# Mamba block of a macaron network: the causal mask of the decay factors moves into spare rows of the cumulative sums' products

## The chip, the cores and the metric

The kernel runs on one core of a Trainium2 chip, in one launch. The metric is the device time of that launch in microseconds (us), taken as the median of three runs. TensorE (PE, with its weight loads PEld), VectorE (DVE), ScalarE (ACT), GpSimd (POOL) and SyncE (SP) each run their own stream of instructions and wait for one another on semaphores. A difference under about 2% is about what these runs can't tell from none.

## The reference

A macaron layer: half a mixture of experts, then a Mamba-2 mixer, then the mixture of experts again, each behind a layer norm and with a residual. The input is 2 x 2048 tokens of width 256. The part that the change touches is the mixer's recurrence over the tokens:

```python
x = x + 0.5 * ffn(layernorm(x))
x = x + mamba2(layernorm(x))      # 8 heads of width 64, state 64
x = x + 0.5 * ffn(layernorm(x))

# inside mamba2, token by token
dA = exp(dt * A)
s = s * dA_t[..., None, None] + dt_t * x_t (outer) B_t
y = einsum('bhpn,bn->bhp', s, C_t)
```

## The kernel before

The program is three blocks behind one another, with a barrier of all engines between two: `ffn_block`, `mamba_block`, `ffn_block`. The change is in `mamba_block` alone, which runs from about 375 us to 905 us of the profiled execution.

`mamba_block` takes the 4096 tokens as 32 tiles (chunks) of 128, in 8 groups of four (`GC = 4`). It computes the recurrence in its chunked form. With `cum` the cumulative sum of `dt * A` within a chunk, the output at token t takes from token s <= t of the same chunk the factor `exp(cum_t - cum_s)` times the product B_s C_t. For each head this factor is a 128 x 128 matrix with s on the partitions and t along the columns, and everything with s > t must vanish.

The order of the work is written out by hand. Each engine has one Python loop `for s in SLOTS` (from -10 to 34), and in slot `s` it works on several tiles at once: TensorE's `within(s)` and `from_state(s)` for tile s, `sums(s + 1, ...)`, `turn_b(s + 1)` and `turn_xc(s + 1)` for tile s + 1, `turn_x(s + 9)` for the normalised input nine tiles ahead. The `project` calls (the five convolution blocks of a group) stand at places that tables give: `EARLY` ones in slots 0 and 1 of every four, ahead of `sums(s + 1, 1)`; `LATE` ones in slots 3, 0 and 1, behind `project_z`. Slots -10 to -1 are a lead-in that only normalises, transposes and projects tiles. Steps hand over by counting semaphores (`Step`), so an engine never runs ahead of what its wait names, and does everything in program order.

The steps that the argument follows:

- `sums(i, half)` on TensorE fills the PSUM bank `pE` for four heads: four products of 128 columns (L1389), whose stationary operand is one column of the selection matrix `pick` broadcast over 128 columns (96 partitions: the high, middle and low bfloat16 parts of 32 rows of cumulative sums in `cumT`), and one product of 512 columns (L1391), an identity times the constant `future`, which adds -1e30 wherever s > t. It runs twice for a tile: `half` 0 at the head of the slot ahead of `from_state`, `half` 1 behind `turn_xc` and an early `project`, ahead of `turn_x` and `turn_y`.
- `decay(i, half)` on ScalarE takes the exponential of `pE` into `ex` (L1245).
- `copy_b(i)` on ScalarE copies the product of B and C and the transposed B into `GB` (L1228).
- `mask(i)` on VectorE multiplies `ex` (all 8 heads, 1024 columns) by that product (L1623). `within(i)` on TensorE then uses `ex` as eight stationary operands (L1340).
- `gate_y(i)` and `add_skip(i)` on GpSimd work on the output `yv` (L1122, L1117), `scale_x` on the inputs of the next tile (L1130 to L1132). `powers(s)` computes `rstd` of the layer norms (L1106); `shift` on VectorE (L1539) and `norm` on ScalarE (L1177) wait for it.
- The start of GpSimd's stream in this block builds the constants with memsets and selects, chained by semaphore waits. TensorE (and VectorE in `prepare`) waits for the last of them, and `powers` stands behind them on GpSimd.
- `softplus(G)` on VectorE is a chain of small operations once for each group (L1569 to L1578), and TensorE's sums over a group (L1476) wait for it.

## Time and profile before

| | us |
|---|---|
| three runs | 1271.49, 1258.30, 1272.85 |
| median | 1271.49 |
| profiled execution: span from first to last instruction | 1265.8 |
| median less that span | 5.7 |
| first `ffn_block`, to the last work of its kind | 0 to 369 |
| `mamba_block` | 375 to 905 |
| second `ffn_block` | 905 to 1265.8 |

The profile has the span of the profiled execution and no other time for it. The stages are read off the timeline of instructions. All durations below come from this one execution.

### The profile page before, as it was taken

How to read it: one execution, taken by the hardware profiler on the slowest of the kernel's cores; microseconds unless marked ns; L12 is line 12 of the kernel's file. 1: busy time of each engine (PE TensorE's matmuls, PEld its weight loads, DVE VectorE, ACT ScalarE, POOL GpSimd, SP SyncE). 2: the span in 40 equal slices, each digit the busy share in tenths (PEclk: the TensorE clock that was granted, in tenths of full speed). 3: DMA queues.
4: the chain of work that ended last, by engine and by line, in shares of the span. 5: the costliest groups of instructions: out<-in, count | busy, mean ns of one | idle time of the engine just before them, and what ended most of it. 6: DMA issues, size and time to landing. Idle time of an engine off the chain costs nothing. (4 is left out here: it accounts for less than half of the span.)

```text
span 1265.8 us, 21732 instructions
## 1 busy us (share of the span) xinstructions
PE 1050.3 (83%) x6532; PEld 870.1 (69%) x6532; DVE 748.1 (59%) x1614; ACT 605.8 (48%) x1560; POOL 607.9 (48%) x612
## 2 busy tenths in 40 slices
PE   3746999999965788989898888989836999999960
PEld 2745999999954556666676666657525999999950
DVE  5974444444427778677878786865355444444437
ACT  1323555555533455556555656565314555555530
POOL 6922555555531245354545454647502555555520
PEclk9997999999985598899989989999858999999985
DMA  7872222322313101111111110000061232222339
GB/s 227 276 294 74 76 76 76 99 76 76 76 59 93 38 30 43 42 42 42 43 42 42 43 38 17 27 17 21 22 279 38 88 97 92 94 95 91 100 117 327
DMA packets 73258, 112.20 MB, mean 89 GB/s; under 512 B 10680, under 2 KB 60352, under 8 KB 71872
## 3 DMA queue, kind: packets, MB, share of 16 engines
q1 hardware_dynamic: 48704, 60.48, 14.2%
q0 software_dynamic: 13824, 37.77, 9.3%
q10 hardware_dynamic: 10624, 12.58, 2.9%
q8 instruction: 61, 1.00, 0.3%
q14 instruction: 45, 0.37, 0.1%
HBM read 66.76 MB, written 44.04 MB: 88 GB/s over the span
## 5 line engine op out<-in xcount | busy, mean ns | idle before, releaser
L427 POOL DMA_INDIRECT ys_d<-xs,row_of x144 | 142.4, 989 | 195.6 <-DVE xs L811 188.2
L422 POOL DMA_INDIRECT xs<-xn_d,token_of x144 | 140.1, 973 | 115.1 <-DVE token_of L785 71.8
L491 ACT ACTIVATE hs<-pH 128x512 f32<-128x512 f32 x144 | 86.0, 597 | 227.6 <-PE pH L613 217.6
L800 DVE TENSOR_TENSOR xl<-pT,xh 128x256 fp32r<-128x256 f32 x144 | 61.1, 424 | 212.7 <-PE pH L613 108.7
L805 DVE TENSOR_TENSOR h2l<-hs,h2h 128x512 fp32r<-128x512 f32 x144 | 99.8, 693 | 81.3 <-ACT h2h L499 77.3
L1604 DVE SCALAR_TENSOR_TENSOR acc<-bank,cwh,acc 128x511 f32<-128x511 f32 (+2 forms) x120 | 89.6, 747 | 40.5 <-ACT acc L1218 37.7
L633 PE MATMUL pY<-w2h,h2h 128*128 x576 | 103.5, 302 | 1.4 <-DVE h2l L805 1.2
L1122 POOL TENSOR_TENSOR yv<-yv,sz 128x512 f32<-128x512 f32 x32 | 40.7, 1272 | 120.6 <-DVE yv L1643 117.4
L613 PE MATMUL pH<-w1h,xh 128*128 x288 | 93.0, 405 | 1.8 <-DVE xl L800 1.1
L613 PE MATMUL pH<-w1l,xh 128*128 x288 | 92.3, 402 | 0.0
L633 PE MATMUL pY<-w2h,h2l 128*128 x576 | 91.1, 280 | 0.0
L613 PE MATMUL pH<-w1h,xl 128*128 x288 | 90.9, 397 | 0.0
L633 PE MATMUL pY<-w2l,h2h 128*128 x576 | 89.5, 278 | 0.0
L497 ACT ACTIVATE hs<-pR 128x512 f32<-128x512 f32 x144 | 87.3, 606 | 4.2 <-PE pR L622 4.2
L499 ACT ACTIVATE h2h<-pR 128x512 fp32r<-128x512 f32 x144 | 89.0, 618 | 0.0
L622 PE MATMUL pR<-ident,hs 128*128 128x128 f32 x576 | 86.3, 272 | 0.0
L633 PEld LDWEIGHTS pY<-w2h,h2h 128*128 128x128 f32 x576 | 78.2, 190 | 2.5 <-issue 2.5
L1106 POOL TENSOR_TENSOR m_rstd<-m_ve,neghalf 128x3 f32<-128x3 f32 x43 | 41.1, 956 | 76.2 <-DVE m_ve L1533 76.2
L633 PEld LDWEIGHTS pY<-w2h,h2l 128*128 128x128 f32 x576 | 77.5, 188 | 0.0
L633 PEld LDWEIGHTS pY<-w2l,h2h 128*128 128x128 f32 x576 | 76.9, 188 | 0.0
L1316 PE MATMUL bank<-wo,yT 128*128 128x256 f32 x256 | 74.0, 440 | 0.0
L1245 ACT ACTIVATE ex<-bank,dts 128x128 f32<-128x128 f32 x256 | 73.3, 380 | 0.6 <-PE bank L1391 0.6
(250 smaller groups left out, 2591.4 us busy)
## 6 DMA issues: line engine op xcount, KB each, us to landing
m_yg<-ys_d SPq DMA_DIRECT2D x64, 128.0 KB, 2.1
xs<-ys_d SPq DMA_DIRECT2D x12, 512.0 KB, 6.8
wst<-in_L_ffn_w_dram ACTq DMA_DIRECT2D x8, 512.0 KB, 4.6
xs<-in_L_attn_x_dram SPq DMA_DIRECT2D x8, 512.0 KB, 6.5
hs<-in_L_ffn_w_dram ACTq DMA_DIRECT2D x8, 512.0 KB, 4.7
xn_d<-xs SPq DMA_DIRECT2D x8, 512.0 KB, 3.4
lo_d<-w1l SPq DMA_DIRECT2D x1, 4096.0 KB, 11.8
lo_d<-w2l SPq DMA_DIRECT2D x1, 4096.0 KB, 21.4
```

What stands on the lines that cost most here:

```text
L422: pool.indirect_dma_start(out=xg[:, t % NX, :], out_offset=None, in_=xn_d, in_offset=bass.IndirectOffsetOnAxis(ap=token_of[:, t:t + 1], ax ...
L427: pool.indirect_dma_start(out=ys_d, out_offset=bass.IndirectOffsetOnAxis(ap=row_of[:, t:t + 1], axis=0), in_=y[:, t % NX, :], in_offset=No ...
L491: act.activation(r[:, u, :], pH[u][:, :], ACT.Relu).then_inc(relu_done.sem, 1)
L497: act.activation(h2[:, u, :, :], turned_h, ACT.Square)
L499: act.activation(h2h[:, u, :, :], turned_h, ACT.Square).then_inc(sq_done.sem, 1)
L613: last = pe.matmul(pH[u][:, :], a[:, u, k, :], w[:, k * HID:(k + 1) * HID], start=(n == 0), stop=(n == 3 * KD - 1))
L622: last = pe.transpose(pR[u][:, k * P:(k + 1) * P], r[:, u, k * P:(k + 1) * P], ident[:, :])
L633: last = pe.matmul(pY[u][:, 0:D], a[:, u, k, :], w[:, k * D:(k + 1) * D], start=(n == 0), stop=(n == 3 * KH - 1))
L805: dve.tensor_tensor(h2l[:, u, :, :], h2[:, u, :, :], h2h[:, u, :, :].bitcast(F32), ALU.subtract).then_inc(h2_split.sem, 1)
L1245: last = act.activation(ex[:, i % 2, h, :], pE[:, n * P:(n + 1) * P], ACT.Exp, bias=dts[:, G % 3, NCUM, k * H + h:k * H + h + 1])
L1316: last = pe.matmul(out, a, b, start=(m == 0), stop=(m == len(parts) - 1))
L1604: ins = dve.scalar_tensor_tensor(a, bank[:, 0:GT - n], cwh[:, b, HALO - n:HALO - n + 1], a, ALU.mult, ALU.add)
```

## The change

The block loses two constants (`ident_bf`, `future`) and the 512-column product L1391. In their place:

- `cumT` gets 32 more partitions, 96 to 127. Row 96 + r holds -1e30 in columns 4r to 4r + 3 and zero elsewhere. They are written once.
- `pick` is no longer 96 x 32 with a broadcast at the time of use, but is written out whole: 128 partitions x 32 selections x 128 columns. In partitions 96 to 127 row r holds one from column 4(r + 1) on. The product of the two thus adds -1e30 where s lies in a later run of four tokens than t, within the same four products of 128 columns.
- What is left to mask are the diagonal 4 x 4 blocks. A new step on GpSimd, `keep_past`, sets the B C product in `GB` to zero where s > t, once for each tile, between `gate_y` of the tile before and `scale_x`. `mask` waits for it.
- `mask` becomes one operation of two stages, the minimum with 3e38 and then the product, since the exponential of an unmasked positive difference could be infinite.

```diff
--- before.py
+++ after.py
@@ -883,6 +883,7 @@
 TAPPED = {0: (1, 0), 1: (1, 2), 2: (1, 4)}
 HANDED = {1: (1, 1), 2: (1, 3)}
 HALO = CONV - 1
+RUN = P // 32
 RX = 14
 LEAD = 10
 
@@ -923,9 +924,8 @@
         heads = sb("heads", [P, 3, H])
         negA, bias = sb("negA", [P, GC, H]), sb("m_bias", [P, GC, H])
         CH = GC * H
-        ident_bf, future = sb("ident_bf", [P, P], BF16), sb("future", [P, GC, P], BF16)
-        pick = sb("pick", [3 * CH, CH], BF16)
-        cumT, rest, mid = sb("cumT", [3 * CH, 2, P], BF16), sb("m_rest", [CH, 2, P]), sb("m_mid", [CH, P], BF16)
+        pick = sb("pick", [P, CH, P], BF16)
+        cumT, rest, mid = sb("cumT", [P, 2, P], BF16), sb("m_rest", [CH, 2, P]), sb("m_mid", [CH, P], BF16)
         xr = sb("xr", [P, RX, D])
         yg = sb("m_yg", [P, 2, TOP, D])
         st, st2 = sb("m_st", [P, 6]), sb("m_st2", [P, 6])
...
@@ -1079,18 +1079,20 @@
         @block.gpsimd
         def _(pool):
             chain = Chain(pool, consts)
-            pool.memset(ident_bf[:, :], 0.0)
-            pool.memset(future[:, :, :], 0.0)
             pool.memset(S[:, :], 0.0)
-            chain.link(pool.memset(pick[:, :], 0.0))
+            chain.link(pool.memset(pick[:, :, :], 0.0))
             for part in range(3):
-                chain.link(pool.affine_select(out=pick[:, :], in_=pick[:, :], compare_op=ALU.not_equal, fill=1.0,
-                                              base=-part * CH, pattern=[[-1, CH]], channel_multiplier=1))
-            chain.link(pool.affine_select(out=ident_bf[:, :], in_=ident_bf[:, :], compare_op=ALU.not_equal, fill=1.0,
-                                          base=0, pattern=[[-1, P]], channel_multiplier=1))
-            chain.link(pool.affine_select(out=future[:, :, :], in_=future[:, :, :], compare_op=ALU.is_ge, fill=-1e30,
-                                          base=0, pattern=[[0, GC], [1, P]], channel_multiplier=-1))
-            for s in (pow_done, xdt_done, xw_done, s1_done, td_done, yv_done, h_ready):
+                chain.link(pool.affine_select(out=pick[0:3 * CH, :, :], in_=pick[0:3 * CH, :, :], compare_op=ALU.not_equal, fill=1.0,
+                                              base=-part * CH, pattern=[[-1, CH], [0, P]], channel_multiplier=1))
+            last = 3 * CH
+            chain.link(pool.memset(pick[last:P, :, :], 1.0))
+            chain.link(pool.memset(cumT[last:P, :, :], -1e30))
+            chain.link(pool.affine_select(out=pick[last:P, :, :], in_=pick[last:P, :, :], compare_op=ALU.is_ge, fill=0.0,
+                                          base=-RUN, pattern=[[0, CH], [1, P]], channel_multiplier=-RUN))
+            for edge, sign in ((0, 1), (RUN - 1, -1)):
+                chain.link(pool.affine_select(out=cumT[last:P, :, :], in_=cumT[last:P, :, :], compare_op=ALU.is_ge, fill=0.0,
+                                              base=edge, pattern=[[0, 2], [sign, P]], channel_multiplier=-sign * RUN))
+            for s in (pow_done, past_done, xdt_done, xw_done, s1_done, td_done, yv_done, h_ready):
                 s.open(pool)
 
             def powers(s):
@@ -1120,6 +1122,11 @@
                 pool.wait_ge(sz_done.sem, sz_done.done(i))
                 pool.wait_ge(t2_done.sem, t2_done.done(i))
                 pool.tensor_tensor(yv[:, :], yv[:, :], sz[:, i % 2, :], ALU.mult).then_inc(yv_done.sem, 1)
+
+            def keep_past(i):
+                pool.wait_ge(bt_done.sem, bt_done.done(i))
+                pool.affine_select(out=GB[:, 0:P], in_=GB[:, 0:P], compare_op=ALU.is_ge, fill=0.0,
+                                   base=0, pattern=[[1, P]], channel_multiplier=-1).then_inc(past_done.sem, 1)
 
             def scale_x(i):
 
@@ -1154,6 +1161,7 @@
                     add_skip(s)
                     gate_y(s)
                 if live(s + 1):
+                    keep_past(s + 1)
                     scale_x(s + 1)
                 if rooted(s + 1):
                     powers(s + 1)
@@ -1308,7 +1316,7 @@
             for s in (xT_ready, x2T_ready, logit_ready, z_ready, dt_ready, cum_ready, p_ready, turned, sm_ready, e0_ready, e1_ready, i_ready, y_ready, s_ready,
                       yT_ready, o_ready):
                 s.open(pe)
-            pe.wait_ge(consts, 6)
+            pe.wait_ge(consts, 9)
 
             def product(out, parts):
 
@@ -1386,10 +1394,9 @@
                     pe.wait_ge(ex0_done.sem, ex0_done.done(i))
                 for n in range(GC):
                     col = k * H + half * GC + n
-                    pe.matmul(pE[:, n * P:(n + 1) * P], pick[:, col:col + 1].to_broadcast([3 * CH, P]), cumT[:, G % 2, :],
-                              start=(n == 0), stop=False, skip_group_check=True)
-                pe.matmul(pE[:, :], ident_bf[:, :], future[:, :, :].rearrange("p h t -> p (h t)"),
-                          start=False, stop=True, skip_group_check=True).then_inc((e0_ready, e1_ready)[half].sem, 1)
+                    last = pe.matmul(pE[:, n * P:(n + 1) * P], pick[:, col, :], cumT[:, G % 2, :],
+                                     start=True, stop=True)
+                last.then_inc((e0_ready, e1_ready)[half].sem, 1)
 
             def turn_x(i):
                 pe.wait_ge(norm_done.sem, norm_done.done(i))
@@ -1487,7 +1494,7 @@
             def prepare():
 
                 dve.wait_ge(loads, 5 * 16)
-                dve.wait_ge(consts, 6)
+                dve.wait_ge(consts, 9)
                 link(dve.tensor_scalar(cwh[:, :, :], cw[:, :, :], 0.5, None, ALU.mult))
                 link(dve.tensor_scalar(cbh[:, :], cb[:, :], 0.5, None, ALU.mult))
                 dve.wait_ge(a_prep, 1)
@@ -1620,7 +1627,9 @@
 
             def mask(i):
                 dve.wait_ge(ex_done.sem, ex_done.done(i))
-                dve.tensor_tensor(ex[:, i % 2, :, :], ex[:, i % 2, :, :], GB[:, 0:P].rearrange("p (a t) -> p a t", a=1).to_broadcast([P, H, P]), ALU.mult).then_inc(M_done.sem, 1)
+                dve.wait_ge(past_done.sem, past_done.done(i))
+                past = GB[:, 0:P].rearrange("p (a t) -> p a t", a=1).to_broadcast([P, H, P])
+                dve.scalar_tensor_tensor(ex[:, i % 2, :, :], ex[:, i % 2, :, :], BIG, past, ALU.min, ALU.mult).then_inc(M_done.sem, 1)
 
             def scale_state(i):
                 dve.wait_ge(i_ready.sem, i_ready.done(i))
```

On GpSimd, at the start of the block (`pick` and `cumT` are the operands of `sums`; m_rstd is what `powers` writes), before:

```order
L1082 MEMSET ident_bf 128x128
L1083 MEMSET future 128x512
L1084 MEMSET S 64x512
L1085 MEMSET pick 96x32
L1087 AFFINE_SELECT pick<-pick 96x32 x3
L1089 AFFINE_SELECT ident_bf<-ident_bf 128x128
L1091 AFFINE_SELECT future<-future 128x512
L1106 TENSOR_TENSOR m_rstd<-m_ve,neghalf 128x3 x9
```

and with the change:

```order
L1082 MEMSET S 64x512
L1083 MEMSET pick 128x4096
L1085 AFFINE_SELECT pick<-pick 96x4096 x3
L1088 MEMSET pick 32x4096
L1089 MEMSET cumT 32x256
L1090 AFFINE_SELECT pick<-pick 32x4096
L1093 AFFINE_SELECT cumT<-cumT 32x256 x2
L1108 TENSOR_TENSOR m_rstd<-m_ve,neghalf 128x3 x9
L1147 TENSOR_TENSOR hc<-hsave,cwh 128x15
```

The selects on `pick` have become selects of 4096 columns, and they stand ahead of the first `powers` as the small ones did.

On GpSimd, in the steady part, one tile's work (`yv` is the output, GB the B C product), before:

```order
L1112 TENSOR_TENSOR S<-S,dts 64x512
L1117 TENSOR_TENSOR yv<-yv,xD 128x512
L1122 TENSOR_TENSOR yv<-yv,sz 128x512
L1130 TENSOR_TENSOR xdt<-xt,dts 128x512
L1131 TENSOR_TENSOR xD<-xt,heads 128x512
L1132 TENSOR_TENSOR xt<-xt,dts 128x512
L1106 TENSOR_TENSOR m_rstd<-m_ve,neghalf 128x3
```

and with the change:

```order
L1114 TENSOR_TENSOR S<-S,dts 64x512
L1119 TENSOR_TENSOR yv<-yv,xD 128x512
L1124 TENSOR_TENSOR yv<-yv,sz 128x512
L1128 AFFINE_SELECT GB<-GB 128x128
L1137 TENSOR_TENSOR xdt<-xt,dts 128x512
L1138 TENSOR_TENSOR xD<-xt,heads 128x512
L1139 TENSOR_TENSOR xt<-xt,dts 128x512
L1108 TENSOR_TENSOR m_rstd<-m_ve,neghalf 128x3
```

One select stands between the gated output and the next tile's scaling.

On TensorE, around the second half of the sums and the head of the next slot (wih, wil and xTh, xTl are the operands of `project` and `project_z`), before:

```order
L1389 MATMUL bank<-cumT,pick 128x128 x4
L1391 MATMUL bank<-future,ident_bf 128x512
L1399 MATMUL bank<-ident,m_xn 128x128 x2
L1408 MATMUL bank<-ident,yv 128x128 x4
L1316 MATMUL bank<-wih,xTh 128x512 x2
L1316 MATMUL bank<-wil,xTh 128x512 x2
L1316 MATMUL bank<-wih,xTl 128x512 x2
L1434 MATMUL bank<-ident,m_xn 128x128 x2
L1389 MATMUL bank<-cumT,pick 128x128 x4
L1391 MATMUL bank<-future,ident_bf 128x512
L1323 MATMUL bank<-S,CT 128x512
```

and with the change:

```order
L1397 MATMUL bank<-cumT,pick 128x128 x4
L1406 MATMUL bank<-ident,m_xn 128x128 x2
L1415 MATMUL bank<-ident,yv 128x128 x4
L1324 MATMUL bank<-wih,xTh 128x512 x2
L1324 MATMUL bank<-wil,xTh 128x512 x2
L1324 MATMUL bank<-wih,xTl 128x512 x2
L1441 MATMUL bank<-ident,m_xn 128x128 x2
L1397 MATMUL bank<-cumT,pick 128x128 x4
L1331 MATMUL bank<-S,CT 128x512
```

The 512-column product is gone from both places; nothing else has moved on TensorE.

## Rows read from the trace of the kernel before

**Rows 1.** page, busy time of each engine, share of the span, instructions

```profile
PE 1050.3 (83%) x6532; PEld 870.1 (69%) x6532; DVE 748.1 (59%) x1614; ACT 605.8 (48%) x1560; POOL 607.9 (48%) x612
```

**Rows 2.** windows by stage: start:end length, busy (x count) per engine, clock, DMA, GB/s

```profile
385.00:430.00 45.00, 30.42 (x105) 23.17 (x104) 34.27 (x97) 15.84 (x38) 7.51 (x13) 0.54 0.23 71
430.00:905.00 475.00, 426.99 (x2335) 311.85 (x2335) 347.95 (x729) 271.79 (x814) 249.94 (x251) 0.94 0.11 34
```

**Rows 3.** waits of TensorE and of its weight loads, 430 to 905 us

```profile
PE bank L1316 <- DVE acc L1604: 19.5, 14, 1.8
PE bank L1408 <- POOL yv L1122: 12.7, 10, 1.8
PE bank L1476 <- DVE dts L1578: 7.6, 6, 1.3
...
PEld bank L1408 <- POOL yv L1122: 20.2, 22, 2.0
```

**Rows 4.** timeline of TensorE, 595 to 606 us

```profile
596.98 0.38 PE L1391 MATMUL bank<-future,ident_bf 128*128 128x512 bf16 x1
597.20 0.38 PE L1399 MATMUL bank<-ident,m_xn 128*128 128x128 f32 x2
...
602.95 0.38 PE L1391 MATMUL bank<-future,ident_bf 128*128 128x512 bf16 x1
603.26 1.12 PE L1323 MATMUL bank<-S,CT 64*128 64x512 f32 x2
```

**Rows 5.** lines L1389, L1391: duration ns min/median/max, first and last start us

```profile
L1389 PEld LDWEIGHTS bank<-cumT,pick x256: 95/98/181, 429.2 to 899.1; 96*128 96x128 bf16 x128
...
L1391 PEld LDWEIGHTS bank<-future,ident_bf x64: 97/97/152, 429.6 to 899.1; 128*128 128x128 bf16 x64
```

**Rows 6.** timeline of GpSimd at the block's start

```profile
375.39 0.20 POOL L1082 MEMSET ident_bf<- 128x128 bf16 x1 [6.17 <-POOLq L113]
375.53 0.52 POOL L1083 MEMSET future<- 128x512 bf16 x1
375.99 0.52 POOL L1084 MEMSET S<- 64x512 f32 x1
376.46 0.12 POOL L1085 MEMSET pick<- 96x32 bf16 x1
376.73 0.21 POOL L1087 TENSOR_SCALAR_AFFINE_SELECT pick<-pick 96x32 bf16<-96x32 bf16 x1 [0.15 <-POOL pick L1085]
...
377.79 0.29 POOL L1089 TENSOR_SCALAR_AFFINE_SELECT ident_bf<-ident_bf 128x128 bf16<-128x128 bf16 x1
378.23 0.64 POOL L1091 TENSOR_SCALAR_AFFINE_SELECT future<-future 128x512 bf16<-128x512 bf16 x1
...
380.80 1.07 POOL L1106 TENSOR_TENSOR m_rstd<-m_ve,neghalf 128x3 f32<-128x3 f32 x1 [1.93 <-DVE m_ve L1533]
```

**Rows 7.** timeline, the first token tile's normalisation reaches TensorE

```profile
381.90 0.16 DVE L1539 SCALAR_TENSOR_TENSOR m_nmr<-m_mv,m_rstd 128x2 f32<-128x2 f32 x1 [0.26 <-POOL m_rstd L1106]
...
383.83 0.58 ACT L1177 ACTIVATE m_xn<-xr,m_nmr,m_rstd 128x256 f32<-128x256 f32 x1
...
384.52 0.66 PE L1399 MATMUL bank<-ident,m_xn 128*128 128x128 f32 x2 [17.01 <-ACT m_xn L1177]
```

**Rows 8.** GpSimd's groups by form, whole span

```profile
L392 POOL IOTA room<- 128x576 f32 x2 | 2.3, 1138 | 0.0
...
L162 POOL TENSOR_SCALAR_AFFINE_SELECT ident<-ident 128x128 f32<-128x128 f32 x1 | 0.3, 292 | 0.2 <-POOL part L157 0.2
```

**Rows 9.** line L1623, same columns

```profile
L1623 DVE TENSOR_TENSOR ex<-ex,GB x32: 1209/1212/1219, 438.5 to 901.8; 128x1024 f32<-128x1024 f32 x32
```

**Rows 10.** line L1616, same columns

```profile
L1616 DVE SCALAR_TENSOR_TENSOR acc<-tb,acc x32: 680/683/1277, 414.5 to 857.1; 128x512 f32<-128x512 f32 x32
```

**Rows 11.** line L1571, same columns

```profile
L1571 DVE TENSOR_TENSOR dts<-dts x8: 192/729/790, 399.8 to 809.1; 128x32 f32<-128x32 f32 x8
```

**Rows 12.** waits of GpSimd, 430 to 905 us

```profile
POOL m_rstd L1106 <- DVE m_ve L1533: 27.8, 21, 2.5
```

More of the change, by code:

```diff
@@ L976, in mamba_block @@
         h_saved, h_ready, h_chain = step("h_saved"), step("h_ready"), sem("h_chain")
-        sm_ready, bt_done, turned, xt_done, e0_ready, ex0_done, e1_ready, ex_done, xdt_done, M_done, xw_done = (
-            step(n) for n in ("sm", "bt", "turned", "xt", "e0", "ex0", "e1", "ex", "xdt", "M", "xw"))
+        sm_ready, bt_done, past_done, turned, xt_done, e0_ready, ex0_done, e1_ready, ex_done, xdt_done, M_done, xw_done = (
+            step(n) for n in ("sm", "bt", "past", "turned", "xt", "e0", "ex0", "e1", "ex", "xdt", "M", "xw"))
         i_ready, y_ready, s_ready, s1_done, S_done, t1_done, td_done, t2_done, yv_done, sq_done = (
```

## The prediction

> **What bounds the kernel now.** The page comes first: TensorE is busy for 1050.3 of 1265.8 us, and no other engine for more than 60% of the span [rows 1]. That is a mean over three blocks, and the change touches only the middle one, so the next view is the windows by stage. In its steady part, 430 to 905 us, TensorE is busy for 427 of 475 us (90%) at a granted clock of 0.94, so mostly the full one of 2.4 GHz; VectorE has 348 us, the others less. In the lead-in before, 385 to 430 us, it is busy for 30 of 45 us at 0.54, so nearly always at 1.2 GHz [rows 2]. Then the waits of TensorE in the steady part: what it waits for longest are three others' chains, a convolution's taps on VectorE (19.5 us in 14 waits), the gated output from GpSimd (12.7 us in 10; its weight loads wait 20.2 us in 22) and the softplus chain (7.6 us in 6) [rows 3]. The steady part is thus TensorE's own program order, with one or two waits in each slot, and a product that is dropped helps only where no such wait follows before the chain that releases it has begun. The fourth view is the timeline at 375 to 385 us, where the block's constants are made while the other engines stand still [rows 6, 7].
>
> **The wide products, removed.** A product of 512 columns is shown as 0.38 us long, but the next one starts 0.22 us behind it (596.98 to 597.20), or 0.31 us at the head of a slot (602.95 to 603.26) [rows 4]. The start distance is what the engine loses, so I price it at 0.22 us; 64 of them make 14.1 us, and with 0.31 at the 32 slot heads 17.0 us. Which of them lie on the path? The 32 of half 1 stand ahead of `turn_x` and `turn_y`. In slots without an early `project` TensorE then waits for the gated output, which started from `within`, ahead of the removed work: the wait grows by what was saved. In slots with an early `project`, the late one waits for the taps of the early one [rows 3]; that chain also starts ahead of half 1. I count half 1 at nothing and say that its cover is these two waits; where one of them is shorter than 0.22 us, a part comes through. The 32 of half 0 stand at the head of the slot, ahead of `out_product`, `within` and `project`, from which those chains start, so what they save shifts everything: 32 x 0.22 = 7.0 us. Bounds: 0 (each is absorbed by some chain of VectorE) and 17.0. I take 7.0.
>
> The four products of 128 columns stay, now with 128 partitions in place of 96 and a written-out operand in place of a broadcast one. The load of the broadcast operand takes 98 ns and that of a full 128 x 128 one 97 [rows 5]; cost nothing, bound 256 x 0.01 = 2.6 us either way. ScalarE's exponentials can begin a little earlier, but ScalarE isn't what is waited for there.
>
> **The constants, made larger.** Before, GpSimd builds them from 375.39 to 378.23 + 0.64 = 378.87 us [rows 6]. Its memsets take 0.20 us for 128 columns and 0.52 for 512, so 0.83 ns a column; its selects 0.29 and 0.64 us for the same, so 0.91 ns a column, and a chained one starts 0.15 us behind the end of the one before [rows 6]. `pick` is now 32 x 128 = 4096 columns in each partition, which gives a memset of 0.20 + 3968 x 0.00083 = 3.5 us and a select of 0.29 + 3968 x 0.00091 = 3.9 us. The new list: memset of `S` 0.5, of `pick` 3.5, three selects 11.7, a memset 3.5, one of 256 columns 0.3, a select 3.9, two of 256 columns 0.8; 24.2 us, and nine chained gaps of 0.15 us make 25.6. It ends at about 401.0 us, 22 us later than before.
>
> All of that stands ahead of the first `powers` on GpSimd. Before, that operation starts at 380.80, when its variance is there, VectorE's shift runs at 381.90, ScalarE's norm at 383.83 and TensorE's first transposition at 384.52 [rows 6, 7]. Now `powers` starts at 401.0, and 1.07 + 0.16 us of it and the shift with hand-overs put the norm at 402.3, so 402.3 - 383.8 = 18.5 us later. Nothing covers it: VectorE stands in program order at the shift, ScalarE at the norm, TensorE at its first transposition, and the loads of further tiles wait for VectorE's adds. In the lead-in the engines already wait for each other in turn (30 of 45 us on TensorE [rows 2]), which is the same chain, only later, so I let nothing be given back. The extrapolation from 512 to 4096 columns is the weak step. Bounds: 10% off the rates, 2 us less; and from above the iota of 576 columns in 1138 ns, 1.98 ns a column [rows 8], which would put 24576 columns x about 1.1 ns = 27 us on top.
>
> The Trainium skill ("GPSIMD Engine Reference", section 3.1) puts a simple loop with at most two operations per element at 1.03 cycles an element; estimated by that page at its 1.2 GHz a pass over 4096 columns is 3.5 us, and the sum would be some 1.6 us lower. The two rows of a select bear the higher price out.
>
> **The new select and the new mask.** `keep_past` on GpSimd is a float32 select of 128 x 128, as that of `ident`, 292 ns [rows 8]; 32 make 9.3 us. Its wait is for ScalarE's copy of the same tile, which is done while GpSimd is still in `gate_y`. Queued behind it are `scale_x` (its product is needed a slot later) and `powers`, which waits for VectorE in 21 of 32 slots anyway, 27.8 us in total [rows 12]; so most of it vanishes there. What remains is VectorE: in the softplus chain a 32-column product of two SBUF operands, 192 ns when alone, has a median of 729 ns [rows 11], because GpSimd is at work; the chain holds TensorE up (7.6 us [rows 3]). I put 8 chains x 0.15 = 1 us, bounds 0 and 9.3 (all 32 on the path). `mask` waits for a select that was done some microseconds before. Its new form has two stages; 512 columns of such a form take 680 ns [rows 10], and 1024 of the old 1212 [rows 9]; the difference, 532 ns for 512 columns, is the one rate of 1.04 ns a column, so the new one takes the same 1.21 us, within 0.05 us: 0, bound 1.6 us.
>
> The Trainium skill ("SBUF — State Buffer", section "Who interferes with whom") says that a VectorE instruction with two SBUF inputs contends with a GpSimd instruction that reads SBUF. By that rule the added select can hold VectorE up in every slot; taken whole it is the third case below, in place of my 1 us.
>
> **The sum.** 18.5 - 7.0 + 1 = +12.5 us. On the profiled span that is 1265.8 + 12.5 = 1278.3; the median of the runs lies 5.7 us above that span, so 1271.5 + 12.5 = 1284.0 us, 1.0% slower. About 2% (25.4 us) is what a measurement of this kernel can tell from no change, so I call it the same, on the slow side.
>
> **The rivals.**
> - Both halves' products come off the path (the waits behind half 1 shrink with it, because their chains were not the later ones): 18.5 + 1 - 14.1 = +5.4, 1277. For it: TensorE is busy 90% [rows 2]. Against it: the waits of [rows 3] stand right behind.
> - GpSimd's new select is on the path in every slot, by holding VectorE up: 18.5 - 7.0 + 9.3 = +20.8, 1292. For it: 192 against 729 ns [rows 11]. Against it: it is 0.29 us in a slot of some 15 us in which GpSimd idles half the time [rows 2].
> - Slower by over 2%: the long passes over `pick` cost more for a column than the short ones, at the iota's 1.98 ns; 12.5 + 27 = +39.5, 1311. It ends above 2% once the six passes take over 1.4 ns a column (12.9 us more over 24576 columns). Against it: 128 and 512 columns are on one line.
> - Not slower: the long passes take under half of my price (some 9 us less in delay) and all 64 products pay: +12.5 - 9 - 7.1 - 2 = -6, 1266. It needs a cheaper form of pass for which no row speaks.
> - The change doesn't drop what it says: on TensorE 64 rows fewer, each a 512-column one, so I give that no weight.
>
> **How the numbers follow.** Chances: forecast 0.55, both halves 0.17, select on the path 0.13, dear passes 0.07, cheap passes 0.05, something else (a different course of the granted clock, which a shorter or longer wait can tip) 0.03. The range takes in the first three with their bounds: from 1277 less 7 (the rest of the 17.0, the 2 us of cheaper passes, and a share of the 14 us between the three runs) = 1270, to 1292 plus 5 (half 0 saving less) = 1297. Over 2% faster is under 1246, for which I have no case: 0.01. Over 2% slower is above 1296.9: dear passes, and the edge of the third case, 0.09. The rest, 0.90, is within 2%.
>
> **What the changed profile would show.** GpSimd's selects on `pick` at 3.9 us each, the last constant at about 401 us, and TensorE's first transposition at 403; 64 products fewer, and a steady part that should be 468 to 470 us long in place of 475, with the wait for the gated output longer by 0.2 us each; `mask` at 1.21 us. I am wrong if the constants end before 390 us or behind 410, if the lead-in comes out shorter than its 45 us, or if the steady part loses more than 12 us or gains any.

## The result, and the profile after

The changed kernel takes 1293.0 us (median of four runs, 1288.28 to 1299.25) against 1264.89 us of the kernel before in its four runs beside it (1257.95 to 1272.85). The ratio is 1.0227, 95% interval 1.017 to 1.0283: 28 us or 2.3% slower, with 2% inside the interval. The forecast was 1284.0 us in a range of 1270 to 1297, 12.5 us above its base. The direction and the range hold, the size is low by more than half, and "within 2%", to which it gave 0.90, is not what the medians say, though the interval leaves it open. Ratios and intervals, here and below, leave out executions that took over 1.5% more than the fastest of their kernel (one each of e1, e5, e9 and e10, and six of e4's twelve); the medians are of all runs.

The profiled execution took 1288.28 us at a span of 1286.6 us, so 1.7 us lie around the span. Of before the span is 1265.8 [rows 1]; the profiled executions differ by 20.8 us. From GpSimd's first memset in it to its last instruction `mamba_block` grew from 550.9 to 574.9 us, and the rest is 3.2 us shorter. (The block's last instruction before ends at 926.3 us and not at 905, where the windows of [rows 2] end.)

First the page of the changed kernel (busy time of each engine, share of the span, number of instructions; the granted clock of TensorE in 40 slices of 32 us), as [rows 1]:

```profile
PE 1032.3 (80%) x6468; PEld 859.4 (67%) x6468; DVE 761.8 (59%) x1614; ACT 605.6 (47%) x1560; POOL 643.6 (50%) x645
PEclk9998999999975799789989999989957999999995
```

TensorE lost its 64 instructions and 18 us of work, and the span grew. VectorE gained 13.7 us of busy time with the same 1614 instructions, so some of them became longer: `mask` by 5.1 us in all, the shift by 3.5, and 4.5 us appear with the long setup alone (e2, 752.6 us). GpSimd gained 36 us in 33 instructions. The slices at 5 are the lead-in (386 to 418 us) and the block's end (933 to 965), as in the kernel before. New is the 7 within the steady part: its slice, 515 to 547 us, has a granted clock of 0.73.

The windows of the changed kernel (columns: start:end, length, busy us and instructions of PE, PEld, DVE, ACT, POOL, granted clock, DMA share, GB/s): part of the lead-in, and the steady part from the first tile's `within` to the 32nd tile's, as [rows 2]:

```profile
407.00:447.00 40.00, 24.72 (x97) 18.29 (x96) 31.09 (x86) 14.64 (x37) 6.67 (x12) 0.64 0.20 59
457.22:930.03 472.81, 409.29 (x2236) 302.76 (x2236) 348.09 (x704) 265.41 (x790) 259.82 (x278) 0.94 0.11 34
```

And of the kernel before, the steady part between the same two products:

```profile
441.77:908.36 466.59, 419.12 (x2297) 306.17 (x2297) 338.75 (x704) 265.45 (x793) 247.18 (x247) 0.95 0.11 34
```

TensorE has 9.8 us less to do in it, and it is 6.2 us longer.

The start of the block in the timeline of the changed kernel, as [rows 6, 7] (start, length, engine, line, operation, output <- inputs, count, what the engine waited for):

```profile
373.87 0.52 POOL L1082 MEMSET S<- 64x512 f32 x1 [6.17 <-POOLq L113]
374.33 3.50 POOL L1083 MEMSET pick<- 128x4096 bf16 x1
377.99 11.91 POOL L1085 TENSOR_SCALAR_AFFINE_SELECT pick<-pick 96x4096 bf16<-96x4096 bf16 x3 [0.15 <-POOL pick L1083]
389.96 3.51 POOL L1088 MEMSET pick<- 32x4096 bf16 x1
...
393.90 3.84 POOL L1090 TENSOR_SCALAR_AFFINE_SELECT pick<-pick 32x4096 bf16<-32x4096 bf16 x1
397.81 0.88 POOL L1093 TENSOR_SCALAR_AFFINE_SELECT cumT<-cumT 32x256 bf16<-32x256 bf16 x2
399.43 0.89 POOL L1108 TENSOR_TENSOR m_rstd<-m_ve,neghalf 128x3 f32<-128x3 f32 x1 [0.74 <-POOL cumT L1093]
400.35 0.16 DVE L1546 SCALAR_TENSOR_TENSOR m_nmr<-m_mv,m_rstd 128x2 f32<-128x2 f32 x1 [14.14 <-POOL m_rstd L1108]
...
400.55 0.60 ACT L1185 ACTIVATE m_xn<-xr,m_nmr,m_rstd 128x256 f32<-128x256 f32 x1 [18.16 <-DVE m_nmr L1546]
...
401.24 0.66 PE L1406 MATMUL bank<-ident,m_xn 128*128 128x128 f32 x2 [35.25 <-ACT m_xn L1185]
```

The block's first memset starts 1.5 us earlier than before, so stages are compared from there. The passes over 4096 columns take 3.50 us (memset) and 3.84 us (select): the forecast's prices. From the block's first memset to TensorE's first transposition it is now 401.24 - 373.87 = 27.37 us; before it was 384.52 - 375.39 = 9.13 [rows 6, 7]. This lengthening of 18.2 us is the largest part of the difference; the steady part adds 6.2, and the earlier start, the lead-in and what follows take 3.7 off.

TensorE's waits in the steady part of the changed kernel (total us, times, longest), as [rows 3]:

```profile
PE bank L1415 <- POOL yv L1124: 23.1, 18, 2.1
PE bank L1324 <- DVE acc L1611: 22.0, 14, 2.0
PE bank L1483 <- DVE dts L1585: 7.3, 5, 1.5
```

The wait for the gated output has nearly doubled, from 12.7 us in 10 to 23.1 us in 18 [rows 3]. It grew by 10.4 us, about what TensorE has less to do. Last the lines that were shown of before (duration in ns, min/median/max), as [rows 9, 5]:

```profile
L1632 DVE SCALAR_TENSOR_TENSOR ex<-ex,GB x32: 1209/1216/2060, 455.2 to 925.0; 128x1024 f32<-128x1024 f32 x32
L1397 PEld LDWEIGHTS bank<-cumT,pick x256: 95/98/181, 446.0 to 922.2; 128*128 128x128 bf16 x128
```

The two-stage mask has the old median, as forecast, but its longest is 2060 ns where it was 1219. The loads of the written-out operand cost what those of the broadcast one did.

### The profile page after: what moved, and what is told of

Same layout as the page of the kernel before. It is cut to its first block and busy times, and to the rows that moved or that the text cites. A ratio compares the mean times of both kernels' runs of the same rounds, so it can differ in the third digit from the quotient of the medians.

```text
span 1286.6 us, 21668 instructions
## 1 busy us (share of the span) xinstructions
PE 1032.3 (80%) x6468; PEld 859.4 (67%) x6468; DVE 761.8 (59%) x1614; ACT 605.6 (47%) x1560; POOL 643.6 (50%) x645
## 5 line engine op out<-in xcount | busy, mean ns | idle before, releaser
L1108 POOL TENSOR_TENSOR m_rstd<-m_ve,neghalf 128x3 f32<-128x3 f32 x43 | 44.2, 1028 | 72.4 <-DVE m_ve L1540 71.5
```

## The experiments

All eleven in one table. The stages are of each profiled execution, in us: start = from GpSimd's first memset of the block to TensorE's first transposition; steady = from the first to the 32nd tile's `within`; at 1.2 GHz = what the granted clock of the windows of 1 us over the steady part adds up to, 2 x (1 - clock) each. The lead-in (55.9 to 57.3 us) and what follows the 32nd `within` (356.0 to 359.2) hardly differ.

| kernel | median (runs) | ratio to before, 95% | span | start | steady | at 1.2 GHz |
|---|---|---|---|---|---|---|
| before | 1264.89 (4) | 1 | 1265.8 | 9.1 | 466.6 | 49.6 |
| changed | 1293.0 (4) | 1.0227, 1.017-1.0283 | 1286.6 | 27.4 | 472.8 | 57.2 |
| e1 constants by ScalarE | 1285.04 (6) | 1.0107, 1.0061-1.0154 | 1296.8 | 9.1 | 496.7 | 123.8 |
| e2 before, long setup | 1283.2 (6) | 1.012, 1.0072-1.0169 | 1279.4 | 28.1 | 462.2 | 33.1 |
| e3 = e1, no select | 1297.56 (7) | 1.0225, 1.0185-1.0265 | 1287.4 | 9.1 | 490.9 | 114.8 |
| e4 before, no wide products | 1278.82 (12) | 0.9977, 0.9927-1.0027 | 1259.8 | 9.1 | 463.5 | 52.9 |
| e5 = e1, wide products dead | 1276.36 (12) | 1.0079, 1.0042-1.0115 | 1273.7 | 9.1 | 474.5 | 53.7 |
| e6 before, waits filled | 1251.98 (6) | 0.9879, 0.9837-0.9922 | 1250.2 | 9.1 | 453.3 | 10.2 |
| e7 = e1, filled | 1255.97 (6) | 0.9904, 0.9867-0.9941 | 1252.9 | 9.1 | 457.3 | 20.5 |
| e8 = e3, filled | 1253.09 (6) | 0.9904, 0.9867-0.994 | 1252.3 | 9.1 | 454.5 | 20.5 |
| e9 = e4, filled | 1252.52 (7) | 0.9906, 0.9874-0.9938 | 1250.1 | 9.1 | 453.9 | 20.4 |
| e10 changed, filled | 1273.45 (12) | 1.0068, 1.004-1.0096 | 1269.6 | 27.4 | 456.1 | 13.7 |
| e11 = e7, select behind | 1253.19 (6) | 0.9906, 0.9871-0.9941 | 1252.3 | 9.1 | 454.3 | 17.0 |

The kernel before ran beside each group: 1272.59 (17 runs, 1260.47 to 1274.2) with e1 to e4, 1266.27 (17) with e5 to e7, 1263.43 (18) with e8 to e11, which ran on another chip. Its own runs are spread over 16 us, largely with the granted clock: in the first group 0.928 of full speed over the whole span in the shortest, 0.912 in the longest. Since its median moves by 9 us from group to group, kernels of different groups are better compared by their ratios, and where the two readings differ both are given. e1's profile was taken of its longest execution (1298.52 us), so its steady part stands for the bad end and not for its median.

**e1, the constants off the path.** GpSimd makes two small tiles, and ScalarE, idle there, writes `pick` out of them; the products' first use waits for the copies.

```diff
-            chain.link(pool.memset(pick[:, :, :], 0.0))
+            chain.link(pool.memset(sel[:, :], 0.0))
...
+            act.wait_ge(consts, 9)
+            act.activation(pick[0:3 * CH, :, :], sel[0:3 * CH, :].rearrange("p (c a) -> p c a", a=1).to_broadcast([3 * CH, CH, P]), ACT.Copy).then_inc(picked, 1)
...
+                if s == -5:
+                    act.activation(pick[3 * CH:P, :, :], runs[3 * CH:P, :].rearrange("p (a t) -> p a t", a=1).to_broadcast([P - 3 * CH, CH, P]), ACT.Copy).then_inc(picked, 1)
...
+                    if i == 0:
+                        pe.wait_ge(picked, 2)
```

> The changed kernel with the operand pick made another way: GpSimd builds only a 96x32 selection and a 32x128 pattern, and ScalarE spreads them over 4096 columns with two copies in its idle time. The steady part is the changed one. Theory (the setup is 18 us of the loss, fully exposed): 17 to 19 us faster than the changed kernel, so the kernel before plus 2 to 10 us, first transposition on TensorE within 1 us of before. Rival (part of the delay is given back in the lead-in or behind it): less than 12 us faster than the changed kernel.

The start is 9.1 us again, so the 18.2 us are the passes over `pick` and nothing else. The median is 1285.0, 8 us under the changed kernel's, but its group was a longer one: by the ratios it is 15 us (0.012 of 1264.9). Neither is the 17 to 19 expected. And it is still 1.1% above before, so something else in the change costs more than the products give.

**e2, the setup alone.** The kernel before, with a tile nobody reads, `dead`, that gets the same passes ahead of `pick`.

```diff
+            chain.link(pool.memset(dead[:, :], 0.0))
+            for part in range(3):
+                chain.link(pool.affine_select(out=dead[0:3 * CH, :], in_=dead[0:3 * CH, :], compare_op=ALU.not_equal, fill=1.0,
+                                              base=-part * CH, pattern=[[-1, CH * P]], channel_multiplier=1))
+            chain.link(pool.memset(dead[3 * CH:P, :], 1.0))
+            chain.link(pool.affine_select(out=dead[3 * CH:P, :], in_=dead[3 * CH:P, :], compare_op=ALU.is_ge, fill=0.0,
+                                          base=0, pattern=[[1, CH * P]], channel_multiplier=-4))
```

> The kernel before, with GpSimd also making the six long passes (two memsets and four selects, 4096 columns) on a tile that nothing uses, ahead of its own constants. Its start is some 3 us longer still than the changed one's, since it keeps its own small constants. Theory (setup exposed): before plus 20 to 22 us. Rival (the lead-in has slack): before plus less than 12 us.

The start is 28.1 us, 19.0 longer. The median went up by 10.6 us only, which by the number is the rival's case; the ratio, 1.012, makes 15 us. Its profiled steady part had 33 us at 1.2 GHz against 50 in the kernel before and is 4.4 us shorter; the lowest runs of that group are 17.3 us apart (1277.8 and 1260.5). So the stage's length is clear, and the medians carry the clock's scatter as well; that the whole of it reaches the end is shown further on, by e7 and e10.

**e3, e1 without the select.** `keep_past` is dropped and `mask` waits for the B C product itself.

```diff
-                    keep_past(s + 1)
...
-                dve.wait_ge(past_done.sem, past_done.done(i))
+                dve.wait_ge(bt_done.sem, bt_done.done(i))
```

> As e1, without the select on GpSimd for each tile (mask waits for ScalarE's copy instead), so the diagonal 4x4 blocks are not masked and the output is wrong there. Theory A (the select moves GpSimd's next three operations 0.3 us later, so that VectorE operations with two SBUF inputs run into them; VectorE's busy time rose 13.7 us): 5 to 9 us faster than e1, VectorE busy time back to about 748 us. Theory B (the loss in the steady part is the granted clock, which falls because TensorE has less work between its waits): within 2 us of e1, dips of the clock in the slots with softplus as in the changed kernel.

Less work than e1 (the diagonal blocks stay unmasked), and a median of 1297.6, 12.5 us longer, which neither theory had. VectorE's busy time is back at 749.7 us, as the first expected, but e1 with its select has 751.2. The three windows of e3 around one place say where it is lost (columns as above; the clock is the third from the end):

```profile
694.00:701.00 7.00, 6.09 (x34) 4.03 (x33) 4.11 (x12) 5.04 (x16) 4.30 (x4) 1.00 0.33 94
701.00:724.00 23.00, 22.10 (x77) 16.54 (x78) 11.47 (x23) 8.62 (x26) 6.46 (x7) 0.55 0.10 30
724.00:730.00 6.00, 4.19 (x23) 3.07 (x22) 4.48 (x7) 4.75 (x16) 1.83 (x2) 1.00 0.00 0
```

For 20.5 us inside the middle window TensorE runs at 1.2 GHz, and no other engine is busy for half of it. From one tile's `within` to the next (from tiles 15, 16 and 17) it took 16.77, 21.43 and 19.73 us there; the same three steps in e4, which has the same products, took 14.34, 16.83 and 15.85, all at full clock. So 23.8 us at 1.2 GHz made them 10.9 us longer. From here on the question is the granted clock.

**e4, the products alone.** The kernel before without the product of 512 columns. It leaves out the masking of s > t; the decay's sign is turned, so that no exponential overflows.

```diff
-                pe.matmul(pE[:, :], ident_bf[:, :], future[:, :, :].rearrange("p h t -> p (h t)"),
-                          start=False, stop=True, skip_group_check=True).then_inc((e0_ready, e1_ready)[half].sem, 1)
+                last.then_inc((e0_ready, e1_ready)[half].sem, 1)
```

> The kernel before, only without its 64 products of 512 columns, so nothing is masked (and the sign of one term is turned, to keep the exponentials finite; the output is not the reference's). Forecast on record: half of them pay, 7 us faster than before. Theory A: the same, 4 to 7 us faster. Theory B (clock): no gain or some us slower, with longer stretches at 1.2 GHz in the steady part than before.

No gain that can be told: the ratio is 0.9977, interval 0.9927 to 1.0027, and it is that of the first two groups below. Its twelve runs fall into three groups by the clock of the whole span: 1260.6 to 1261.9 us at 0.924, 1274.8 and 1275.1 at 0.911, 1282.6 to 1284.5 at 0.894 to 0.900. The best group is no faster than the best runs of the kernel before (1260.5), and the last one is slower than any of them.

**e5, the products given back as dead ones.** e1, with the 512-column product ahead of the four in each half; its result is overwritten.

```diff
+                if half in (0, 1):
+                    pe.matmul(pE[:, :], pick[:, 0, :], pick[:, 0:GC, :].rearrange("p h t -> p (h t)"), start=True, stop=True)
```

> As e1, with the 64 wide products put back as dead work: 512 columns of bfloat16 ahead of the four products of each half, written to the same bank and overwritten. Theory C (the loss in the steady part is TensorE's clock: without the wide products TensorE waits longer behind the same VectorE chains and is granted 1.2 GHz more often): 5 to 15 us faster than e1 although it does more, within 5 us of the kernel before, 30 to 60 us at 1.2 GHz between the first and the last tile in place of 124. Rival (the select or the two-stage mask costs): as e1 or up to 7 us slower than e1.

64 products more than e1, and a median 8.7 us lower (1276.4 against 1285.0). By the ratios it is 3.5 us (1.0079 and 1.0107) with intervals that overlap, so all that e5 shows is that giving the work back costs nothing; and it is not within 5 us of the kernel before, as expected. Whether dead work can make the kernel faster is for the next run.

**e6, TensorE's waits filled.** The kernel before, with dead products just ahead of TensorE's three long waits of [rows 3], each behind a short wait of its own: four ahead of `turn_y` in slots 2 of every four, five ahead of the late `project` in slots 0 and 1, four ahead of the sums over a group.

```diff
+            def idle_products(out, n):
+                for _ in range(n):
+                    pe.matmul(out, ident_bf[:, :], future[:, :, :].rearrange("p h t -> p (h t)"), start=True, stop=True)
...
+                if live(s) and live(s + 1) and s % GC == 2:
+                    pe.wait_ge(xt_done.sem, xt_done.done(s + 1))
+                    idle_products(pT[:, :], 4)
...
+                if live(s) and live(s + 1) and s % GC in (0, 1) and blocks(s, LATE):
+                    pe.wait_ge(ex_done.sem, ex_done.done(s + 1))
+                    idle_products(pE[:, :], 5)
...
+                if G is not None and live(s) and live(s + 1):
+                    pe.wait_ge(ex_done.sem, ex_done.done(s + 1))
+                    idle_products(pE[:, :], 4)
```

> The kernel before, with dead products of 512 bfloat16 columns in three of TensorE's waits of every four slots: 4 ahead of the gated output's transposition in the slot without a project, 5 ahead of each late project in the next two, 4 ahead of the sums over a group. Each fits in a wait of 1.3 to 1.8 us. Theory C: next to no time at 1.2 GHz in the steady part (under 20 us), 5 to 15 us faster than before, and the runs lie closer together. Rival (the clock follows something else): no change of the clock, time as before or a few us slower.

1251.98 us, 1.2% faster than the kernel before. TensorE's timeline in e6 shows the filled places:

```profile
590.99 1.25 PE L1439 MATMUL bank<-future,ident_bf 128*128 128x512 bf16 x5
592.40 0.69 PE L1316 MATMUL bank<-xTh,wih 128*128 128x512 f32 x2 [0.16 <-DVE acc L1617]
...
604.22 1.04 PE L1439 MATMUL bank<-future,ident_bf 128*128 128x512 bf16 x4 [0.75 <-ACT xt L1233]
605.28 0.66 PE L1408 MATMUL bank<-ident,yv 128*128 128x128 f32 x4
```

Dead work of 1.25 us stands where the wait for the taps was, and what is left of the wait is 0.16 us. The late `project` begins when its operand is there, as before. TensorE's waits over e6's steady part:

```profile
PE bank L1408 <- POOL yv L1122: 5.8, 8, 1.1
...
PE bank L1489 <- DVE dts L1591: 2.1, 6, 0.4
...
PE bank L1316 <- DVE acc L1617: 1.6, 10, 0.2
```

And the window of e6's steady part:

```profile
440.64:893.98 453.34, 426.64 (x2393) 302.87 (x2423) 341.70 (x704) 265.35 (x793) 247.72 (x247) 0.99 0.11 35
```

The wait for the taps went from 19.5 us to 1.6, the granted clock from 0.95 to 0.99, the stretches at 1.2 GHz from 49.6 us to 10.2, and the steady part from 466.6 to 453.3 us. Step by step (from one tile's `within` to the next), the nine steps that such a stretch touches before and not in e6 are 15.2 us shorter; the steps at full clock in both are equal to 0.05 us, save two (from tiles 8 and 20), which before follow a lengthened step and are 0.73 us shorter there. So the gain is the clock's.

**e7, e1 filled; e10, the changed kernel filled.** The same filler, with `pick` as both operands. e7 was expected without the fill at the sums over a group; the kernel has it, as e6 does.

> As e1, with the same dead products in the waits as e6, and without those at the sums. Theory C: under 20 us at 1.2 GHz in the steady part, as fast as e6 or up to 3 us faster, 15 to 25 us faster than e1. Rival (select and mask cost something of their own): 5 us or more slower than e6 at the same clock.

> The changed kernel itself, with the dead products in the waits. Against e7 this prices the long setup at a steady clock: 18 to 19 us slower than e7, 1274 us. Against the changed kernel it shows what its clock costs: 12 to 20 us faster.

e7 takes 1255.97 us, 29 us less than e1 (26 by the ratios), but 4.0 more than e6, where up to 3 us less was expected; e10 takes 1273.45, 19.5 less than the changed kernel. Between the two stands the setup alone (with ScalarE's two copies in e7): 17.5 us by the medians, 16.7 by the spans, 20.7 by the ratios (0.0164 of 1264.9), with starts that are 18.3 us apart. At a nearly even clock (20.5 and 13.7 us at 1.2 GHz) the constants' passes reach the end in full.

**e8, e3 filled, and e9, e4 filled.**

> As e7 (small constants, dead products in the waits) without the select for each tile; the diagonal 4x4 blocks are not masked. Theory A2 (at the full clock the select itself costs: it moves GpSimd's next operations into VectorE's mask and shift, whose means rose from 1240 and 222 ns in e6 to 1346 and 421 ns in e7): 3 to 5 us faster than e7, mask mean back to 1240 ns, slots with softplus back to about 15.1 us from 16.1. Rival (the slots with softplus are longer for the missing wide products or the two-stage mask): as e7 within 1 us.

> As e6 without the 64 wide products, nothing masked and one sign turned as in e4. This prices the removed products alone at a steady clock. Forecast on record: 7.0 us faster than with them. Theory D (VectorE leads the slots, so only the last slots and a few others pay 0.22 us): 1 to 3 us faster than e6.

e8 takes 1253.09 us, 2.9 under e7; it is taken up with e11. e9 against e6 is the product's removal: 1252.52 and 1251.98 us, ratios 0.9906 and 0.9879, so the removal of 64 products brings no time; 1 to 3 us was expected. The clock is similar but not equal, 20.4 us at 1.2 GHz in e9's steady part against 10.2. The steps between one `within` and the next tell the two apart (us, profiled executions; a choice of the 25 steps that no stretch at 1.2 GHz touches in either):

| step from tile | e6, with the products | e9, without |
|---|---|---|
| 16 | 17.04 | 16.82 |
| 17 | 15.86 | 15.85 |
| 18 | 13.27 | 13.27 |
| 19 | 15.33 | 15.33 |
| 22 | 12.24 | 12.24 |
| 24 | 15.18 | 15.18 |
| 27 | 10.93 | 10.72 |

The step from tile 16 is the distance of two rows of `within` in TensorE's timeline, first in e6:

```profile
687.20 1.90 PE L1340 MATMUL bank<-xdt,ex 128*128 128x64 f32 x16
704.24 1.90 PE L1340 MATMUL bank<-xdt,ex 128*128 128x64 f32 x16
```

and in e9:

```profile
686.40 1.90 PE L1340 MATMUL bank<-xdt,ex 128*128 128x64 f32 x16
703.22 1.89 PE L1340 MATMUL bank<-xdt,ex 128*128 128x64 f32 x16
```

Eight steps (from tiles 8, 13, 16, 20 and 26 to 29) get shorter by 0.21 to 0.24 us, about the price of the one product at the head of the slot; there TensorE is the chain. That makes 1.8 us, which e9's longer stretches at 1.2 GHz hide. In 15 others the step is the same to 0.02 us: its length comes from the others' chains, and both halves' products only fed a wait. (The two left, from tiles 3 and 5, are shorter in e9 by 1.1 and 0.4 us, but follow steps that a stretch had lengthened.)

**e11, the select moved behind `scale_x`.**

```diff
-                    keep_past(s + 1)
                     scale_x(s + 1)
+                    keep_past(s + 1)
```

> As e7, with the select behind the three operations of scale_x in place of ahead of them. Theory A2: the three operations no longer start later, so half or more of the select's cost goes: 2 to 4 us faster than e7. Rival (any 0.29 us on GpSimd costs the same): as e7 within 1 us.

1253.19 us, that of e8 without a select in the same group (1253.09). With the select ahead of `scale_x` (e7) the median is 2.8 us and the steady part 3.0 us longer, the span 0.6; the ratios to the kernel before are equal, so the time alone doesn't settle it. A second comparison, within one group, is e10, select ahead and long setup, against e11: 20.3 us, of which the start explains 18.3. VectorE's groups by form over the whole span show what the place of the select does; columns: count | busy us, mean ns | idle before. First e7:

```profile
L1652 DVE SCALAR_TENSOR_TENSOR ex<-ex,GB 128x1024 f32<-128x1024 f32 x32 | 43.1, 1346 | 0.0
L1566 DVE SCALAR_TENSOR_TENSOR m_nmr<-m_mv,m_rstd 128x2 f32<-128x2 f32 x43 | 15.7, 365 | 1.2 <-POOL m_rstd L1109 1.2
```

And the same two groups of e11:

```profile
L1652 DVE SCALAR_TENSOR_TENSOR ex<-ex,GB 128x1024 f32<-128x1024 f32 x32 | 39.0, 1218 | 9.1 <-POOL GB L1129 9.1
L1566 DVE SCALAR_TENSOR_TENSOR m_nmr<-m_mv,m_rstd 128x2 f32<-128x2 f32 x43 | 10.6, 247 | 1.2 <-POOL m_rstd L1109 1.2
```

With the select ahead, `mask` has a mean of 1346 ns and the shift 365; with it behind, 1218 and 247, though `mask` now waits 9.1 us in all for the select. What happens in the bad case stands in the timeline of the changed kernel. GpSimd's rows:

```profile
631.79 0.29 POOL L1128 TENSOR_SCALAR_AFFINE_SELECT GB<-GB 128x128 f32<-128x128 f32 x1
632.05 1.04 POOL L1137 TENSOR_TENSOR xdt<-xt,dts 128x512 f32<-128x512 f32 x1
633.06 1.04 POOL L1138 TENSOR_TENSOR xD<-xt,heads 128x512 f32<-128x512 f32 x1
634.06 1.49 POOL L1139 TENSOR_TENSOR xt<-xt,dts 128x512 f32<-128x512 f32 x1
635.51 1.84 POOL L1108 TENSOR_TENSOR m_rstd<-m_ve,neghalf 128x3 f32<-128x3 f32 x1
```

And VectorE's at the same time:

```profile
634.57 2.06 DVE L1632 SCALAR_TENSOR_TENSOR ex<-ex,GB 128x1024 f32<-128x1024 f32 x1
```

The select itself is 0.29 us and runs alone. But it pushes the three products of `scale_x` behind it, and the last one now runs into `mask`: 1.49 us in place of 1.04 on GpSimd, 2.06 in place of 1.21 on VectorE, and `powers` 1.84 in place of 0.89. Six of the 32 masks in the changed kernel are of that length, none before [rows 9]. They are those of tiles 3, 7, 11, 15, 19 and 27, so all in the slots where the softplus chain runs. How often the operations meet also hangs on the course of the slots: e7 has five such masks and e11 none, but e8 without a select has two, and e1 with the select ahead has no more than e3 without it, two each.

What this costs can be read at full clock within one group, in the step from tile 7, ahead of which nothing is lengthened either: 16.40 us with the select ahead (e10), 15.69 with it behind (e11), 15.34 without it (e8). From tile 19 it is 15.90 in e10 and 15.33 in e8. Behind `scale_x` the select is cheaper, then, and not free; that the medians of e11 and e8 agree is within their scatter of 5 to 7 us.

## Why the prediction was right in direction and low in size

The filled kernels give each part at a similar clock. Their differences are good to some 3 us: e7 and e8, which did not run in one group, are 2.9 us apart by medians, 2.8 by steady parts, 0.6 by spans and equal by ratios.

- **The setup, 18.5 us: right.** The start grew by 18.2 us in the changed kernel and by 19.0 in e2; 16.7 to 20.7 us reach the end between e7 and e10. Passes, their prices, the first transposition (forecast 403, measured 401.24 with the block begun 1.5 us earlier) and "nothing covers it" all held. The extrapolation from 512 to 4096 columns, called the weak step, was good to 0.1 us a pass. The Trainium skill ("GPSIMD Engine Reference", section 3.1) puts a simple loop at 1.03 cycles an element, which makes, as an estimate, 3.5 us for such a pass. The memsets agree (3.50 us), the selects take 3.84, and the trace decides for the higher one.
- **"What they save shifts everything: 32 x 0.22 = 7.0 us": the step that failed.** It assumed that what stands ahead of `out_product`, `within` and `project` on TensorE is on the path in every slot, since those chains start from them. The steps of e6 and e9 are equal in most slots: there a TensorE that is through 0.22 us sooner waits 0.22 us longer for a chain of the others. At full clock eight steps pay, 1.8 us in all in place of 7.0, and the times show none of it (e4 -3 us +- 6, e9 against e6 +0.5 us by medians and +3.4 by ratios): the bound of 0 that the forecast gave. That half 1 pays nothing was right: of the steps that can be compared none got shorter by two products.
- **The select, 1 us with bounds 0 and 9.3: low, and by another operation.** It is 0 to 3 us, 3 by the steady parts of e7 and e8 and 2 by what e10 has over e11 beyond the start; single steps at full clock lose 1.1 and 0.6 us (from tiles 7 and 19). The forecast looked for it in the softplus chain. The slots were right, but it acts there by what it pushes into `mask` and the shift. The Trainium skill ("SBUF — State Buffer", section "Who interferes with whom") says that such a pair contends; the trace agrees, with 2060 ns beside 1219. Behind `scale_x` it costs 0.1 us by the medians (e11 against e8) and a third of the price in the step from tile 7 (0.35 of 1.06 us), so what is paid is mostly the place and not the work.
- **The new mask form and the full operand, 0: right.** Median 1216 against 1212 ns, loads of 98 ns, and e8 against e9 (select-free, new forms) 0.6 us.
- **"the median of the runs lies 5.7 us above that span": true of these runs, but nothing to build on.** Around a span lie 1.7 us in each kernel, so the profiled execution of before was one of about 1267.5 us. The base of 1271.5 was the median of three runs that scatter over 15 us, and beside the changed kernel it came out as 1264.9. That 1293.0 fell into the range is therefore in part luck: set around 1264.9, the same range ends at 1290.4.
- **The granted clock, left out of the sum and put at 0.03: the rest of the miss.** The miss is 15.6 us, 28.1 measured against 12.5. At a nearly even clock the change costs 21.5 us (e10 less e6; by the ratios 23.9): 18.3 of the start and some 3 of the steady part, where the select costs more than the products give. Some 9 of the 15.6 us (by the ratios 11) are thus the products and the select, and some 7, by the ratios 5, the clock: filling the waits brings the changed kernel down by 19.5 us and the kernel before, by its ratio, by 15.

Of its own signs of being wrong one came true: the steady part, which was to be 5 to 7 us shorter and not to gain any, is 6.2 us longer.

How longer waits become a slower clock can be read at one place of TensorE's timeline of the changed kernel:

```profile
642.40 0.39 PE L1406 MATMUL bank<-ident,m_xn 128*128 128x128 f32 x2
644.20 0.66 PE L1415 MATMUL bank<-ident,yv 128*128 128x128 f32 x4 [1.41 <-POOL yv L1124]
...
647.50 0.38 PE L1441 MATMUL bank<-ident,m_xn 128*128 128x128 f32 x2
649.31 0.41 PE L1483 MATMUL bank<-dts,incl_tri 128*128 128x32 f32 x2 [1.44 <-DVE dts L1585]
649.65 0.41 PE L1484 MATMUL bank<-incl_tri,dts 128*32 128x128 f32 x2
```

and in its windows around that place:

```profile
640.00:650.00 10.00, 7.15 (x40) 4.78 (x39) 9.52 (x28) 6.15 (x17) 5.11 (x6) 1.00 0.22 66
650.00:656.00 6.00, 6.00 (x20) 3.99 (x20) 4.63 (x7) 1.66 (x8) 2.55 (x3) 0.58 0.00 0
656.00:668.00 12.00, 10.91 (x62) 8.44 (x61) 8.24 (x23) 6.43 (x18) 5.44 (x6) 0.93 0.19 57
```

Two waits of 1.41 and 1.44 us stand within 7 us, TensorE is busy for 7.15 of 10, and right behind the second wait the clock falls from 1.00 to 0.58: TensorE is then busy without a pause for 6 us on 20 products. The step of that slot took 18.32 us, 16.14 in the kernel before, where the clock fell too, behind a single wait of 1.30 us, but for 3.4 us of the step and not 5.7; about 1 us of the difference is the long mask of tile 11 (the step at full clock is 15.57 us in e10 and 14.55 in e11). Every us dropped ahead of a wait lengthens it; a stretch at 1.2 GHz falls on work that does bind, and costs some half of its length (10.9 us for 23.8 in e3's three steps). That the waits are the cause is shown by e6, e7 and e10, which add nothing but dead products in them. (In the changed kernel's steady part no wait is over 2.3 us and the clock falls ten times; in e6 all waits but one are under 1.1 us and it falls three times.) That it was the removed products that made the waits longer fits the 23.1 us in place of 12.7, but no run separates it from the shifts that the select and the setup bring. Which execution gets how many such stretches was not foreseen by any kernel here: e1, e3 and e4 have runs of one kernel 11 to 24 us apart. Why e3 lies so steadily at the bad end while e4, with the same instructions on TensorE, goes both ways stays open.

The Trainium skill ("TensorE: Matmul & The Clock Gate", section "A second HAM failure mode: psum-queue depth-cycling") says that short idle times between groups of products, where they are frequent, are enough to make the clock swing between its two levels; by that rule the change could lose from removing work, and these rows agree.

Of the rivals, "both halves" and "cheap passes" fell with e9 and the timeline, "dear passes" with 3.50 and 3.84 us. "Select on the path in every slot", +20.8 us, has the number that the profiled spans gave, but not the reason: its 9.3 us are 3 at most. The fastest kernel of all is e6, the kernel before with its waits filled, at 1251.98; the change in its best form, constants by ScalarE, select behind, waits filled (e11), is at 1253.19, so it brings nothing that can be measured.

## What to carry to other kernels

Price a removed instruction by the wait behind it: where a steady part is a ring of chains, equal steps from one landmark to the next with and without the instruction are the test, and the answer can be 2 us for 64 products that keep the engine busy for 18. On TensorE look at the granted clock before taking work off it, and try dead products in its waits of 1 to 2 us, behind a wait that comes earlier: that alone gave 1.2% here, more than the change could have. Constants that grow by writing out a broadcast are paid in full when they stand ahead of the first step of a block; another engine that idles there can write them, and a small added step goes where what it pushes back meets nobody.

## What the hardware showed that was not expected

- The granted clock can turn a saving into a loss: without 18 us of TensorE's work and without the long setup the ratios to before were 0.998 (e4), 1.011 (e1) and 1.023 (e3), and with the waits filled 0.991, 0.990 and 0.990 (e9, e7, e8); adding 126 dead products of 512 columns, 32.0 us busy, to the changed kernel (e10) took 1.5% off.
- One kernel's runs come in groups by clock: e4 at 1261, 1275 and 1284 us, with 0.924, 0.911 and about 0.897 over the span.
- GpSimd's passes over bfloat16 go by columns and not by partitions: the memset of 4096 columns takes 3.50 us on 128 partitions and 3.51 on 32, the select 3.84 us on 32 and 11.91 for three on 96.
- A float32 operation of 1024 columns on VectorE goes from 1.21 to 2.06 us when one of 512 columns on GpSimd runs into its start, and GpSimd's own go from 1.04 to 1.49 and from 0.89 to 1.84 us.
